# Adding matrix products that nobody reads behind the stages of the edge passes of a four-layer GNN kernel

## Time and profile before

| | |
|---|---|
| median of three runs | 10778.5 us (10772.28 to 10779.0) |
| profiled execution | 10698.97 us, span 10697.2 us, mean granted TensorE clock 0.653 |
| busy PE / PEld / DVE / ACT / POOL | 45% / 34% / 40% / 17% / 61% |
| chain that ended last, by engine | unknown queue 36%, issue 21%, PE 21%, DVE 11%, POOL 4% |
| gathers of the typed passes (L776, typed_table) | 3128, 2997.6 us busy, 1569.8 us idle before them |
| gathers of passes 1 and 2 (L776, node_table) | 2835, 2732.4 us busy, 1753.7 us idle before them |

### The profile page before, as it was taken

One profiled execution on the slowest core, in us unless ns is written; L12 is line 12 of the kernel. 1 busy time (PEld: TensorE's weight loads), 2 busy tenths in 40 slices (PEclk: granted clock), 3 DMA queues, 4 the chain that ended last, 5 costly groups with the idle time before them and its releaser, 6 DMA issues.

```text
span 10697.2 us, 122041 instructions
## 1 busy us (share of the span) xinstructions
PE 4797.8 (45%) x31058; PEld 3606.8 (34%) x31058; DVE 4232.9 (40%) x8620; ACT 1862.9 (17%) x5090; POOL 6552.4 (61%) x6391
## 2 busy tenths in 40 slices
PE   3788455555555457777777411211112311211111
PEld 3677444444444435555555211111111111111110
DVE  7899544445444554444444211212212111211212
ACT  0677223223322200000000100000000100000000
POOL 8333466666666545666665466666666566666666
PEclk9999655555555578898889655555555655555555
DMA  6000133333333312222222222222222222222222
GB/s 262 23 15 15 38 87 89 89 88 90 89 89 88 80 45 64 64 64 65 64 64 65 81 58 56 60 55 59 59 54 59 87 56 59 58 57 57 58 58 55
DMA packets 491880, 728.06 MB, mean 68 GB/s; under 512 B 143188, under 2 KB 206036, under 8 KB 488933
## 3 DMA queue, kind: packets, MB, share of 16 engines
q0 software_dynamic: 204288, 216.96, 11.8%
q1 hardware_dynamic: 159948, 245.16, 7.3%
q10 hardware_dynamic: 127584, 265.22, 6.5%
HBM read 421.77 MB, written 305.03 MB: 68 GB/s over the span
## 4 chain that ended last, share of the span: by engine, by line
another core or an unknown queue 36%; issue 21%; PE 21%; DVE 11%; POOL 4%; ACT 3%; DVEq 2%; DMA 2%; ACTq 0%; SPq 0%; POOLq 0%
PE ps L1672 8%; PE ps L1736 3%; DVE scn L1328 2%; PE ps L1704 2%; PE ps L1581 2%; PE ps L1548 1%; DVE shared L1308 1%; POOL big L723 1%; PE ps L1553 1%; DVE idx L1293 1%; POOL big L786 1%; DMA flags<-keep_and_type_rows 1%; DVE picked_nodes L1267 1%; POOL gat L776 1%
## 5 line engine op out<-in xcount | busy, mean ns | idle before, releaser
L776 POOL DMA_INDIRECT gat<-typed_table,idx x3128 | 2997.6, 958 | 1569.8 <-issue 918.2
L776 POOL DMA_INDIRECT gat<-node_table,idx x2835 | 2732.4, 964 | 1753.7 <-issue 857.7
L1736 PE MATMUL ps<-ident,scn 128*128 128x128 f32 x3136 | 938.3, 395 | 3543.4 <-DVE scn L1328 2335.8
L1328 DVE TENSOR_TENSOR_SCAN scn<-flags,scn,ps 128x256 f32<-128x256 bf16 x1176 | 874.0, 743 | 3510.1 <-remote 2966.3
L1736 PEld LDWEIGHTS ps<-ident,scn 128*128 128x128 f32 x3136 | 566.8, 226 | 3843.3 <-issue 3825.9
L863 ACT COPY dmp<-ps 128x256 f32<-128x256 f32 x1568 | 586.6, 374 | 6316.6 <-remote 3885.0
L1672 PE MATMUL ps<-big 128*128 128x320 bf16 x8820 | 1454.7, 319 | 147.1 <-issue 73.4
L1672 PEld LDWEIGHTS ps<-big 128*128 128x128 bf16 x8820 | 915.5, 104 | 550.3 <-issue 179.3
L1704 PE MATMUL ps<-ident,gat 128*128 128x128 f32 x3136 | 888.3, 380 | 443.2 <-DVE gat L1298 299.0
L1721 PE MATMUL ps<-shared,bd_w 128*128 128x256 f32 x784 | 447.6, 673 | 988.8 <-issue 596.2
L1704 PEld LDWEIGHTS ps<-ident,gat 128*128 128x128 f32 x3136 | 529.6, 193 | 558.9 <-issue 507.1
(11 more groups left out here) (287 smaller groups left out, 6087.5 us busy)
## 6 DMA issues: line engine op xcount, KB each, us to landing
scan_rows<-dmp ACTq DMA_DIRECT2D x784, 256.0 KB
flags<-keep_and_type_rows SPq DMA_DIRECT2D x980, 128.0 KB
spread_table<-tsl ACTq DMA_DIRECT2D x101, 576.0 KB, 15.9
shared<-spread_table SPq DMA_DIRECT2D x196, 288.0 KB
gat<-typed_table,idx POOLq DMA_INDIRECT x3128
gat<-node_table,idx POOLq DMA_INDIRECT x2835
typed_table<-shared SPq DMA_DIRECT2D x20, 1280.0 KB
group_rows<-node_group_rows SPq DMA_DIRECT2D x98, 128.0 KB
```

Of the source, the lines that this page charges most:

```text
L776: nc.gpsimd.indirect_dma_start(gat[:, k, g // ST, g % ST, :], None, table[:, :], bass.IndirectOffsetOnAxis(ap=idx[:, k, g:g + 1], axis=0)) ...
L1328: v.tensor_tensor_scan(scn[:, 1 - b, :], kept, values, scn[:, b, SH - 1:SH], ALU.mult, op).then_inc(s_scan, 1)
L1736: last = nc.tensor.transpose(bank(2 + b1)[:, g * P:g * P + P], by_edge(scn[:, b1, :], g), ident[:, :])
```

## The change

PE gets a helper `fill(times)`, which issues so many float32 products of the identity with itself into bank 7. They wait for nothing, raise no semaphore, and nobody reads bank 7 in these passes. `FILL` gives the number for each pass: three in pass 1, none in pass 2, six in passes 3 and 4. The helper is called behind the first transposes, in the MLP pass also behind the second stage, and behind the transposes back. So a typed step gets 12 products and a step of the MLP pass 9.

```diff
+FILL = (0, 3, 0, 6, 6)
...
+                def fill(times):
+                    for _ in range(times):
+                        nc.tensor.matmul(bank(7, P), ident[:, :], ident[:, :], start=True, stop=True)
...
                         last.then_inc(s_turn, 1)
+                    fill(FILL[q])
                     multiply_some(s, c, k, live, range(0, 4 if mlp else 5))
...
                         last.then_inc(s_wsum, 1)
                     if mlp:
+                        fill(FILL[q])
                         multiply_some(s, c, k, live, range(4, 7))
...
                         last.then_inc(s_back, 1)
+                    fill(FILL[q])
                     multiply_some(s, c, k, live, range(7 if mlp else 5, JA))
```

## The result

The changed kernel takes 11095.88 us (11078.44 to 11104.21), beside it the kernel before 10777.24 us (10772.28 to 10779.0): ratio 1.0297, 95% interval 1.0283 to 1.0312, so 319 us or 3.0% slower. The profiled execution took 11098.65 us, 400 us more than the profiled one of before; that one lay 80 us under its own median, this one 3 us over. So some 80 of the 400 us between the two profiles are not in the medians.

The account below looks back on a forecast made before the run. POOL's pauses, waiting for PE's late handover, were taken as the bound. Typed passes lose 300 to 650 us, MLP 70 to 220; the middle, 620, on 10778.5 gives about 11400 us, own range 11150 to 11650.

Parts of the forecast that it names:

- The bound: Typed and MLP passes: POOL sets the pace, and only its pauses, 0.72 and 1.03 us a step, can change.
- The handover is late whatever PE does: PE's results reach DVE and ACT late while POOL gathers, with or without products behind them; scans still wait several us.
- The cure: Rival: products behind PE's transposes carry results out and POOL's pauses go, at most 968 us faster; chance 0.28, whole or half.
- Each record counts: Every PE record is finished late while POOL gathers, so 28 typed and 32 MLP records a step bring more pauses.
- the line: POOL's pauses a step grow by 0.0115 for each PE record: 0.50 typed, 0.55 in the MLP pass.
- the reading of 1.5 us a record: Between passes 1 and 2, 15.4 us between two reads hold ten PE records, taken as 1.5 us late each.
- The price of a pause: A POOL pause costs 2.2 to 3.1 us typed, 2.2 to 2.9 us MLP; the middle sum was 620 us slower.
- the small loss: Rival between hidden products and forecast: only the price of the bursts counts, 50 to 370 us slower; chance 0.07.
- PE's price and the clock: A product costs PE 0.44 or 0.24 us by clock; typed clock rises from 0.52 to 0.7 or more, without gain.
- PE became no bound: Rival: PE's own work bounds typed and MLP steps at 6.2 and 7.4 us, 1660 us slower; chance 0.13.
- The lateness of the products themselves: The added products on PE, like every record, were taken to be finished late, in order, while POOL gathers.
- Everything else: No reader, wait or queue is touched; products behind the end of each pass cost some 20 us at most.

Follow-up runs that it names:

- e5: The kernel before, without an edit, run again on a second chip where handovers are prompt: 9252.07 us, ratio 1.0001.
- e11: Kernel before with twelve short bfloat16 products behind each stage of pass 3, and half of the transposes left out in pass 4, late chip: 10923.83 us, ratio 1.0096.
- e12: Kernel before with three 512-column float32 products a step in pass 3, and iotas replacing pass 4's gathers, prompt chip: 8866.99 us, ratio 0.9573.
- e9: Changed kernel with twelve products behind each typed stage in place of six, none in the MLP pass, prompt chip: 9912.59 us, ratio 1.0715 to the kernel before.
- e6: The changed kernel, without an edit, on the second prompt chip: 9288.06 us, ratio 1.0041 to the kernel before.

## Why the prediction was right or wrong, point by point

**The bound: right.** What was lost, was lost in POOL's pauses. Of the typed step's 0.35 us, 0.31 are pauses.

**The handover is late whatever PE does: right in what it said of the change, unproved in its cause.** With products behind every stage DVE's scans still stand idle, once for 12.05 us and on average for 4.90 us a step (1216.4 / 248), before 4.56 (1198.8 us for 263 scans in the window of the earlier trace rows). The cure, to which I gave 0.28, did not come. That POOL's gathers cause it can't be the whole: the prompt chips gather at the same pace (947 ns and 0.30 us between two in e5, 955 and 0.29 in the earlier trace rows) and hand over at once. Nor is it late whatever PE does: in pass 4 of e11, on a late chip with POOL gathering, PE with half of its records handed over to ACT at once, and DVE was slow instead. The chip or its state and PE's work both have a part; whether the gathers have one isn't settled (e12), and how these come together stays open. The readings of the earlier trace rows, on which I built, hold for the chip of the profile alone.

**Each record counts: the pauses rise with the records on late chips, but the line is rough and the reading of 1.5 us a record was wrong.** By POOL's idle gaps of over 0.6 us, the typed passes had 0.22 pauses a step with 4 records, 0.27 with 12, 0.42 with 28, 0.38 with 28 of which 24 short, and 0.24 with 2; the MLP pass 0.38 with 14, 0.50 with 32, 0.84 with 50. By the line I had 0.50 for 28 records and 0.55 for 32. A record more adds 0.008 in the one pass, 0.006 and then 0.019 in the other. Nor did each record delay the handover by the 1.5 us of the earlier trace rows: over both typed passes a scan starts 9.7 us on average after its transposes in the kernel before, with 4 records a step, and 4.2 us after them in the changed one, with 28 (4.5 us in e5, where nothing is late and only DVE's order makes it wait). The forecast took only the count from that reading, so that it came out in the right direction has luck in it. Whether the count itself or the time that goes with it matters, e11 leaves undecided.

**The price of a pause: the term that was mis-sized.** I had 2.2 and 3.1 us as ends and took the middle for 0.50 pauses. Measured were 0.45 waits of 2.4 us, together 1.09 us a step (1.03 by the idle time) where my middle was 1.33; as gaps of over 0.6 us they are 0.42 of 2.6 us, the same product, so how much of the miss is number and how much is price depends on the way of counting. The price isn't a constant between two ends; by either count it falls as the pauses become more frequent. By the waits it is 3.1 us at 0.22, 2.8 at 0.31, 2.4 at 0.45, 2.1 at 0.76. In the rows I had the same fall between the earlier trace rows. Taking pass 2's price for pass 2's frequency would have given 1.10 - 0.72 = 0.38 us a typed step and 1.21 - 1.03 = 0.18 in the MLP pass, 370 us. Measured: 0.35 and 0.15, which is 333 us with 784 and 392 steps in two profiles that are 400 us apart, and 319 in the medians. So the low end of my sum was nearer than its middle of 620 us. The time fell 54 us under my forecast's own range, into what I had called the small loss, and the typed step of 6.05 us just under the 6.1 to 6.5 that I had named as a sign, though POOL's pauses rose as forecast.

**PE's price and the clock: nearly right, and without weight.** 0.22 us a product at the higher clock (e9), 0.24 forecast. PE was busy for 366 of 500 us, over the 250 asked for, and the clock rose from 0.52 to 0.80, over 0.7. PE became no bound. The Trainium skill ("TensorE: Matmul & The Clock Gate", section "Why this matters for your kernels") advises to avoid idle gaps so that the clock stays up; the clock of 0.80 agrees, and the time of 3% more, or 0.4% more on a prompt chip, shows what it is worth where PE isn't the bound.

**The lateness of the products themselves: not foreseen.** I had them finished late; the timeline of the result shows them start late, with 1.0 us between records that wait for nothing. A stage behind such records starts late too. Over both typed passes the first transposes start 0.26 us on average after DVE's scaling in the kernel before and 6.6 us after it in the changed one; the scan then follows 9.7 and 4.2 us later. So the delay behind the transposes was more than halved, in part what the rival of the cure had said, but the delay in front of them took more: from scaling to scan it is 10.1 us before and 11.0 after (4.9 on a prompt chip, e5). That is the path by which the products cost more pauses; that they do it by their number isn't shown. The same page, section "The mechanism", has matmuls start in order, and the timeline agrees: the transposes back of 7037.54 start behind the twelfth product, of 7037.43.

**Everything else.** I had 20 us at most. The gathers that became longer are not in it: 13 ns each, 0.05 us a step or 40 us in the typed passes, and 26 ns in the MLP pass of a prompt chip. Some 30 us of the profile lie outside the gathers' rows and were not traced further.

No version that does the whole work beat the kernel before on its own chip.

## What to carry to other kernels

An engine that pauses and shows the lower clock loses nothing by it as long as another engine sets the pace: here a clock of 0.50 and one of 0.96 gave the same 5.00 us a step. Work without a reader is not free on an idle engine either; ask what it does to those who wait for that engine's results, and price such a wait at the frequency that you expect, not in the middle of two others. Count pauses by the idle gaps themselves, not by the waits that a view names. And when a profile shows waits that no instruction accounts for, run the unchanged kernel on another chip before building on them: here it took 1525 us less there.

## What the runs showed of the hardware that was not expected

- The same kernel takes 9252 us on one chip and 10708 to 10826 us on others. On the kind that takes longer ScalarE reads TensorE's results 7.3 us on average after the start of the last transpose (typed passes of the profile before), on the other kind 0.5 us (e5). Records of TensorE that wait for nothing often stand 1.0 to 1.1 us apart there, where they otherwise follow each other in 0.112 us (e9). Whether it is the chip or its state isn't known.
- The delay isn't bound to TensorE. With half of its transposes, on such a chip, ScalarE reads them 0.6 us on average after their start, but VectorE is idle for 1.2 us and more in front of operations that wait for nothing, and its sequencer's register operations take 0.70 us at the median in place of 0.07 (passes 4 and 3 of e11). The held-up records of TensorE come 0.7, 1.4 or 2.1 us after each other, too.
- An indirect DMA of 128 rows takes GpSimd 957 ns beside TensorE's work of the MLP pass, 983 ns when nine more products a step are added; in the typed pass 947 ns without and 945 ns with twelve more, and 980 ns with 24 more (group of 616 in e9), when PE is busy all the time.
- In a full stretch a float32 product of 128 columns costs 0.22 us of PE (two records of 0.112 us), less than the 0.285 us would suggest that the groups show as the mean of one record in shorter bursts (e6).
